# Another order of the calls on five engines, in a kernel of attention and experts on one core of Trainium2

## The reference

```python
xn = layernorm(x)
# attention: 32 query heads, 8 key/value heads, head size 128
q, k, v = heads(xn @ Wq.T), heads(xn @ Wk.T), heads(xn @ Wv.T)
q, k = q * cos + rotate_half(q) * sin, k * cos + rotate_half(k) * sin
attn = softmax(where(causal, q @ k.T / sqrt(128), -inf)) @ v
# experts: 16 of them in 4 groups, the best 2 groups, in them the best 2 experts
s = softmax(xn @ router_w + router_b) + router_bias
gate = scores of the 2 chosen experts, 0 for the others
ffn = sum_e gate_e * ((silu(xn @ w1_e + b1_e) * (xn @ w2_e + b2_e)) @ w3_e + b3_e)
shared = (silu(xn @ sw1 + sb1) * (xn @ sw2 + sb2)) @ sw3 + sb3
out = x + attn @ Wo.T + ffn + shared
```

## Time and profile before

| | |
|---|---|
| median of 3 runs | 904.24 us (903.93 to 904.62) |
| the profiled execution | 904.18 us |
| its span | 902.4 us |
| TensorE busy | 880.4 us, 98% |
| VectorE / POOL / ScalarE busy | 689.3 / 521.7 / 425.6 us |
| chain that ended last, by engine | PE 73%, DVE 9%, issue 5%, DMA 5%, POOL 4% |
| heads, us from the span's start | 74.2, 164.8, 271.2, 377.2, 483.4, 589.6, 695.2, 802.3, end 902.4 |

### The profile page before, as it was taken

How to read it: one execution, slowest core, us unless ns; L and a number is a source line. 1 busy time by engine, 2 the same in 40 slices (tenths; PEclk the granted TensorE clock), 3 DMA queues, 4 the chain that set the end, 5 groups by cost and what they waited for, 6 DMA issues and landing times.

```text
span 902.4 us, 17525 instructions
## 1 busy us (share of the span) xinstructions
PE 880.4 (98%) x5086; PEld 752.5 (83%) x5086; DVE 689.3 (76%) x1615; ACT 425.6 (47%) x1082; POOL 521.7 (58%) x638
## 2 busy tenths in 40 slices
PE   8997999999999999999999999999999999999987
PEld 7786887888888888888888888888888878888766
DVE  5587877777677877778777787778867696787976
ACT  3504544454545544554454455454454554544542
POOL 5915776547554576545754476545756447644564
PEclk9998999999999999999999999999999999999999
DMA  9911122244222532225322343225423153221153
GB/s 332 318 47 47 36 93 94 95 130 140 82 72 76 173 109 85 88 66 178 98 87 79 120 146 102 76 76 152 127 76 87 64 192 99 87 65 48 40 147 106
DMA packets 52161, 97.73 MB, mean 108 GB/s; under 512 B 5920, under 2 KB 17824, under 8 KB 52128
## 3 DMA queue, kind: packets, MB, share of 16 engines
q1 hardware_dynamic: 49568, 88.94, 31.1%
q0 software_dynamic: 2560, 8.39, 2.9%
HBM read 74.76 MB, written 22.54 MB: 108 GB/s over the span
## 4 chain that ended last, share of the span: by engine, by line
PE 73%; DVE 9%; issue 5%; DMA 5%; POOL 4%; ACT 2%; SPq 1%; POOLq 0%; DVEq 0%; ACTq 0%
PE bank L1891 8%; PE bank L1893 8%; PE bank L1892 8%; PE bank L2118 5%; PE bank L2025 5%; PE bank L2122 5%; PE bank L2119 5%; PE bank L2027 5%; PE bank L2026 5%; PE bank L2086 4%; PE bank L2099 3%; PE bank L2102 3%; PE bank L2100 3%; DMA w_raw<-w 2%; POOL prob L586 1%
## 5 line engine op out<-in xcount | busy, mean ns | idle before, releaser
L586 POOL TENSOR_SCALAR prob<-prob,rsum 128x128 f32<-128x128 f32 (+3 forms) x256 | 141.6, 572 | 137.0 <-DVE rsum L1405 136.8
L812 ACT ACTIVATE prob<-bank,nmax 128x128 f32<-128x128 f32 (+3 forms) x256 | 133.6, 528 | 105.8 <-DVE nmax L1399 100.5
L1399 DVE CUSTOM_DVE_ANT_0 bank<-bank,causal 128x128 f32<-128x128 f32 (+3 forms) x256 | 121.0, 507 | 35.3 <-PE bank L1893 26.1
L832 ACT ACTIVATE pT_hi<-bank 128x512 fp32r<-128x512 f32 x160 | 91.6, 596 | 91.6 <-PE bank L2086 76.8
L1427 DVE TENSOR_TENSOR pT_lo<-bank,pT_hi 128x512 fp32r<-128x512 f32 x160 | 105.3, 682 | 26.8 <-ACT pT_hi L832 24.0
L535 POOL TENSOR_TENSOR q_first<-rot 128x128 f32<-128x128 f32 x60 | 28.6, 476 | 138.8 <-DVE rot L1355 138.8
L2025 PE MATMUL bank<-xT_hi,wq_lo 128*128 128x512 f32 x256 | 103.3, 403 | 1.8 <-DVE kT_lo L1390 1.5
L2118 PE MATMUL bank<-wo_lo,oT_hi 128*128 128x512 f32 x256 | 102.8, 402 | 1.7 <-DVE y L1420 1.4
L2027 PE MATMUL bank<-xT_hi,wq_hi 128*128 128x512 f32 x256 | 101.0, 395 | 0.0
L2122 PE MATMUL bank<-wo_hi,oT_lo 128*128 128x512 f32 x256 | 100.9, 394 | 0.0
L2026 PE MATMUL bank<-xT_lo,wq_hi 128*128 128x512 f32 x256 | 100.9, 394 | 0.0
(11 more groups left out here) (219 smaller groups left out, 2341.6 us busy)
## 6 DMA issues: line engine op xcount, KB each, us to landing
w_raw<-w SPq DMA_DIRECT2D x31, 512.0 KB, 4.3
wq_raw<-wq SPq DMA_DIRECT2D x32, 256.0 KB, 2.7
wo_raw<-wo SPq DMA_DIRECT2D x32, 256.0 KB, 3.0
xg<-x_slots SPq DMA_DIRECT2D x31, 256.0 KB, 3.6
w_raw<-w SPq DMA_DIRECT2D x31, 256.0 KB, 2.6
eb<-b SPq DMA_DIRECT2D x31, 256.0 KB, 3.8
y_slots<-eb SPq DMA_DIRECT2D x31, 256.0 KB, 2.4
x_slots<-pairs SPq DMA_DIRECT2D x3, 2048.0 KB, 16.5
```

The costliest lines, as they stand in the source:

```text
L586: last = nc.gpsimd.tensor_scalar(row, row, rsum[:, stat(b, i, h)], 1.0, ALU.mult, ALU.mult)
L812: last = nc.scalar.activation(prob[n % 2][:, h, 0:P * (i + 1)], bank[S_BANKS[use % 2]][:, 256 * k:256 * k + P * (i + 1)], ACT.Exp, bias=nm ...
```

## The change

The same calls stand in another order. In SyncE's and POOL's lists first_head and key_head change (of POOL's last_head the first few calls), in ScalarE's, VectorE's and TensorE's all three lists. No call is added or taken away: key_head has 158 calls on TensorE, 136 on VectorE, 95 on ScalarE, 39 on SyncE and 35 on POOL in both; arguments, buffers and semaphores are the same. The diff, cut to the places that follow:

```diff
@@ POOL, first_head
                         gather(n, 1)
 
             def first_head(g):
-                place_x(g, 0)
                 normalise(g, 0, 0)
                 normalise(g, 0, 1)
                 add_k(g, 1, 0)
                 add_q(g, 1, 0)
                 add_k(g, 1, 1)
+                place_x(g, 0)
+                add_q(g, 1, 1)
                 normalise(g, 0, 2)
-                add_q(g, 1, 1)
+                normalise(g, 0, 3)
...
@@ VectorE, first_head
             def first_head(g):
                 maxima(g, 0, 0, 0)
-                first_places(g, 0)
                 maxima(g, 0, 0, 1)
                 turn_k(g, 1, 0)
+                first_places(g, 0)
                 lo_v(g, 1, 0)
+                maxima(g, 0, 1, 0)
                 inverse_sums(g, 0, 0)
-                maxima(g, 0, 1, 0)
                 maxima(g, 0, 1, 1)
-                lo_wo(g, 0)
+                inverse_sums(g, 0, 1)
                 turn_q1(g, 1, 0)
-                turn_q2(g, 1, 0)
-                inverse_sums(g, 0, 1)
-                lo_wo(g, 1)
-                lo_wo(g, 2)
                 maxima(g, 0, 2, 0)
                 maxima(g, 0, 2, 1)
+                turn_q2(g, 1, 0)
+                maxima(g, 0, 2, 2)
+                maxima(g, 0, 2, 3)
+                lo_wo(g, 0)
                 lo_pT(g, 0, 0, 0)
                 turn_k(g, 1, 1)
+                lo_wo(g, 1)
...
@@ VectorE, key_head
                 lo_pT(g, 0, 1, 1)
-                add_b12(tile_of(g, 1))
-                lo_q(g, 1, 0)
-                maxima(g, 0, 3, 1)
+                lo_xg(tile_of(g, 1))
+                add_out(g - 1, 1, 3)
+                turn_q1(g, 1, 1)
+                turn_q2(g, 1, 1)
                 lo_wo(g, 0)
                 lo_wo(g, 1)
+                add_b12(tile_of(g, 1))
+                maxima(g, 0, 3, 0)
                 expert_product(tile_of(g, 1))
-                turn_q1(g, 1, 1)
-                turn_q2(g, 1, 1)
                 expert_hidden(tile_of(g, 1))
-                add_out(g - 1, 1, 3)
-                maxima(g, 0, 3, 2)
-                lo_kT(g, 1)
-                lo_hT(tile_of(g, 1))
-                lo_q(g, 1, 1)
-                lo_pT(g, 0, 2, 0)
-                maxima(g, 0, 3, 3)
-                add_b3(tile_of(g, 1))
-                lo_oT(g, 0, 1)
                 lo_wo(g, 2)
                 lo_wo(g, 3)
+                lo_hT(tile_of(g, 1))
+                lo_pT(g, 0, 2, 0)
...
@@ VectorE, last_head
-                lo_pT(g, 0, 3, 1)
-                lo_oT(g, 0, 2)
                 maxima(g, 1, 3, 3)
-                add_out(g, 0, 1)
+                combine_two(g, 0)
+                inverse_sums(g, 1, 3)
                 maxima(g, 1, 2, 0)
-                inverse_sums(g, 1, 3)
                 lo_pT(g, 0, 3, 2)
                 maxima(g, 1, 2, 1)
                 lo_pT(g, 0, 3, 3)
-                combine_two(g, 0)
                 maxima(g, 1, 2, 2)
-                maxima(g, 1, 2, 3)
+                add_out(g, 0, 2)
                 lo_oT(g, 0, 3)
                 lo_pT(g, 1, 3, 0)
                 lo_pT(g, 1, 3, 1)
-                add_out(g, 0, 2)
+                maxima(g, 1, 2, 3)
+                combine_two(g, 1)
                 inverse_sums(g, 1, 2)
                 lo_pT(g, 1, 3, 2)
-                combine_two(g, 1)
+                maxima(g, 1, 1, 0)
                 lo_pT(g, 1, 3, 3)
-                lo_pT(g, 1, 2, 0)
-                maxima(g, 1, 1, 0)
                 maxima(g, 1, 1, 1)
                 lo_oT(g, 1, 3)
+                lo_pT(g, 1, 2, 0)
                 lo_pT(g, 1, 2, 1)
+                inverse_sums(g, 1, 1)
                 add_out(g, 0, 3)
-                inverse_sums(g, 1, 1)
                 maxima(g, 1, 0, 0)
+                lo_pT(g, 1, 2, 2)
                 maxima(g, 1, 0, 1)
-                lo_pT(g, 1, 2, 2)
                 combine_two(g, 2)
                 lo_oT(g, 1, 2)
```

More of the change, by code:

```diff
@@ L1661, in key_head @@
                 maxima(g, 0, 2, 2)
+                lo_pT(g, 0, 0, 0)
+                lo_oT(g - 1, 1, 3)
                 maxima(g, 0, 2, 3)
[L1663 to L1668 removed]
+                add_out(g - 1, 1, 2)
+                turn_k(g, 1, 1)
+                lo_q(g, 1, 0)
+                inverse_sums(g, 0, 2)
+                lo_v(g, 1, 1)
@@ new lines, in key_head @@
+                transpose_p(g, 0, 3, 3)
+                project_out(g, 0, 2, 0)
+                project_out(g, 0, 2, 1)
+                project_out(g, 0, 2, 2)
+                scores(g, 1, 1, 0)
+                scores(g, 1, 1, 1)
+                expert_down(tile_of(g, 2))
+                project_out(g, 0, 2, 3)
+                project_q(g + 1, 0, 0, 0)
+                project_q(g + 1, 0, 0, 1)
+                transpose_x(tile_of(g, 3))
+                transpose_p(g, 1, 0, 0)
+                values(g, 0, 3, 2)
```

1143 lines of the change are left out of this document (565 added, 578 removed).

## The result

The changed kernel takes 892.82 us (median of 4 runs, 891.38 to 896.03) where the kernel before, in the same measurement, takes 904.09 (902.66 to 904.62): ratio 0.9883, 95% interval 0.9853 to 0.9912, 11.3 us faster. I had forecast 902.1, with a range from 897.5 to 907.5. The profiled execution has a span of 890.6 us.

What follows compares the result with a forecast made beforehand. TensorE was taken as the bound, busy 880.4 of 902.4 us, leaving at most 22.0 us to reordering. 904.18 + 0.4 (first head) - 0.6 (six passes) - 1.9 (last head) = 902.1 us, range 897.5 to 907.5.

Steps and rivals of the forecast that it cites:

- The first head, +0.4: First head: later lo_v and new waits slightly outweigh taking POOL's scatters off normalise's path; +0.4 us, ends -1.5 and +2.
- The six passes, -0.6: Six middle passes: two waits go, smaller ones come; -0.1 us each, -0.6 in sum.
- the two waits of the middle pass: Middle pass: TensorE's waits for kT_lo (0.40 us) and pT_lo (0.44) go, 0.84 in sum.
- transpose_h(1): Middle pass, tile 1: 5.6 us of matmuls against a VectorE chain of 5.35; 0.3 us taken, 1.1 if one lo_wo is stretched.
- transpose_x(4): Middle pass, tile 4: stands 3.8 us behind what it needs against a chain of 3.65; 0.35 us (0 to 0.7).
- expert_down(0): Middle pass, tile 0: a new lateness of 0.1 us.
- a term that I had put at nothing: Middle pass: merging transpose runs saves nothing, with 13 runs before and after by the orders.
- theory D: Follow-up theory, not in the prediction, on key_head: where TensorE's calls stand (distance) sets the pass, whatever VectorE's operations take.
- rival C: Passes: VectorE falls behind, lo_wo stretched beside POOL's add_q(1,1), from 0.25 us on; 907.2 us, chance 0.25.
- Rival B: Passes: separating VectorE from POOL's subtracts removes every wait, -0.84 us each, idle under 0.2; 897.7 us, chance 0.17.
- The last head, -1.9: Last head: moved combines let inverse_sums(1,1) and normalise come earlier, emptying project_out's 1.36 us wait; -1.9 us.
- Rival D: Whole kernel: nothing gained, the 1.36 us wait moves and passes exchange waits; 904.2 us, chance 0.20.

Runs made afterwards that it cites:

- before_again: The kernel before once more, unchanged: 905.46 us.
- kt_swap: The kernel before with one TensorE swap in key_head, project_q(g,1,2,0) behind expert_down(1): 904.8 us.
- three_more: The changed kernel with three places mended (VectorE's row slots, one project_kv piece, inverse_sums and normalise(1,3) earlier): 887.9 us, ratio 0.9832 to the kernel before.
- pool_hit: The changed kernel with one POOL swap in key_head, lo_w3(1) behind add_q(1,1): 897.24 us.
- key_no_pool: The kernel before with key_head in the new order on four engines, POOL's list kept as before: 942.05 us.
- pool_free: The kernel before with one POOL swap in key_head, lo_w3(2) ahead of split_q(g+1,0): 903.7 us.
- key_only: The kernel before with only key_head in the new order, on all five engines: 898.46 us.

## Why the prediction was wrong

**The first head, +0.4.** Its steps came nearly as written: lo_v ended 0.9 us later, 2.60 us behind turn_k's start where it was 1.69 (at 81.90 in the profile after), the scatters left the path, and one short wait for normalise(0,1) came (0.41, and one of 0.26 in batch 1). Rows of after, to be laid beside the earlier trace rows:

```profile
80.04 0.28 DVE L1319 SCALAR_TENSOR_TENSOR place<-per_expert,bank 128x128 f32<-128x128 f32 x1
...
81.48 0.42 DVE L1383 TENSOR_TENSOR v_lo<-bank,v_hi 128x256 fp32r<-128x256 f32 x1
...
81.95 0.50 PE L2025 MATMUL bank<-xT_hi,wq_lo 128*128 128x512 f32 x1 [1.25 <-DVE v_lo L1383]
...
82.92 1.42 POOL L586 TENSOR_SCALAR prob<-prob,rsum 128x128 f32<-128x128 f32 x4 [7.77 <-DVE rsum L1405]
...
86.95 0.36 PE L2086 MATMUL bank<-ident,prob_t 128*128 128x128 f32 x2 [0.41 <-POOL prob L586]
```

Measured, it is the same as the profile before (90.5 for 90.6 us), and 1.8 less than that order takes on average. What failed is the size of the wait for normalise behind the scatters: I took it from one execution, and that was one of the two in which it was shortest. The granted clock goes with it. From the head's start to the first of these transposes, in the profile before and in before_again:

```profile
74.18:88.01 13.83, 11.47 (x57) 10.20 (x57) 9.41 (x34) 7.71 (x23) 7.45 (x10) 0.75 0.16 66
72.16:86.24 14.08, 10.04 (x57) 8.79 (x57) 10.47 (x36) 7.60 (x23) 7.70 (x10) 0.88 0.16 65
```

Where TensorE ran at 1.2 GHz for 6.8 us of it (before, kt_swap) it came later to the transposes and waited 1.0 us; where it ran so for 3.4 (the six other profiles with the old first head) it waited 2.8 to 3.4 us. Without the wait TensorE would have come 12.1 us behind the head's start in before_again and 13.1 in the profile before: 1.0 of the 1.7 us by which the waits differ.

**The six passes, -0.6.** This is the step that failed. Measured: 106.4 to 105.2, -1.2 a pass, 5.9 us in the five that can be compared, a little over half of the result. It failed in three places. What goes: I counted the two waits of the middle pass, 0.84 us. In the seven profiles of the old key_head the pass also has waits for wo_lo of up to 0.9 us and for kT_lo of up to 0.94 (start to start, above the usual distance), that come and go from pass to pass, and they went too. What comes: I took 0.3 for transpose_h(1), 0.35 for transpose_x(4) and 0.1 for expert_down(0), 0.75 in all. The first two did not come. The third is the one that did, and it costs 0.43 from start to start (lo_hT of tile 0 behind turn_q2(1,0)):

```profile
283.64 0.68 DVE L1355 TENSOR_TENSOR rot<-bank,qs 64x512 f32<-64x512 f32 x1
...
284.36 0.29 DVE L1497 TENSOR_TENSOR hT_lo<-bank,hT_hi 128x128 fp32r<-128x128 f32 x1
...
284.80 0.47 PE L1891 MATMUL bank<-w_hi,hT_lo 128*128 128x512 f32 x1 [0.27 <-DVE hT_lo L1497]
```

The third place is a term that I had put at nothing. I had counted 13 runs of transposes of probabilities before and after; the trace has 13 before (seven of eight, six of four) and 12 after (eight of eight, four of four), and that isn't all. With every wait that the table lists taken out at its length from start to start, a pass of the old order still takes 105.3 to 105.6 us in its seven profiles, one of the new order 104.7, and three_more, whose passes have no such wait, takes 104.8. So 0.5 to 0.9 of the 1.2 us a pass, an estimate, are in no wait of the table. Part of it lies between short matmuls of different kinds: in the profile before transpose_k begins at 361.09, 0.25 us behind the transpose ahead of it, and the second of the scores at 275.58 is 0.18 behind the first, where 0.09 and 0.11 are usual and the middle pass after has nothing longer. This is theory D's side, the places of TensorE's calls; no run takes it apart from the rest.

The two errors on the waits have one root: I had VectorE as stretched after as before. The chain that I reckoned for transpose_h, 5.35 us against 5.6, holds undisturbed; and it was nearly undisturbed.

```profile
299.94 1.56 DVE L1455 TENSOR_TENSOR wo_lo<-wo_raw,wo_hi 128x512 fp32r<-128x512 f32 x2
...
299.99 0.96 POOL L535 TENSOR_TENSOR q_first<-rot 128x128 f32<-128x128 f32 x1 [0.38 <-DVE rot L1355]
...
302.36 0.28 DVE L1480 SCALAR_TENSOR_TENSOR gated<-both_in 128x128 f32<-128x128 f32 x1
...
303.02 0.14 PEld L2167 LDWEIGHTS bank<-ident,h_rows_t 128*128 128x128 f32 x1 [0.17 <-DVE h_rows L1490]
```

This is rival C's place, and it went the other way: VectorE and POOL start at the same signal, VectorE is 0.05 us ahead, and it is POOL's L535 that takes 0.96 us for 0.46; the two lo_wo lose 0.2 us together, under the 0.25 from which C decides. pool_hit shows that C's price was of the right size (1.1 us a pass, once the product is the one that comes second) and its condition not met. Rival B, with 0.17, comes nearest: the stretches beside POOL went from 31.4 to 10.5 us and the waits for pT_lo and kT_lo with them. But its sign, under 0.2 us idle a pass, wasn't met (0.27), and its -0.84 a pass is too small and holds waits alone. How much of the 1.2 us is due to the meetings is not shown: by what is left without the waits they can have about half, key_no_pool mixes two causes, and pool_free shows that a single meeting can be taken away for nothing.

The rule of the Trainium skill that I had set beside row 312.23 ("SBUF — State Buffer", section "Who interferes with whom"), that the engine which comes second is shut out for the whole instruction, is what the 57 stretched operations do. For descriptor writing, which is what a gather does on POOL, the same section infers that it needs another interface than such an operation of VectorE takes; here the gathers took 1.01 us and beside combines 1.21 to 1.63. My reading, that exclusion would cost four whole combines and that the row at 882.77 therefore doesn't agree, was wrong: in the 14 profiles 68 gathers began while such an operation of VectorE ran, and 66 of them ended at its end plus their own shortest 1.01 us, less 0.03 to 0.13. A gather waits for the rest of the one combine that it meets, 0.65 us at 882.77. The other way round there is nothing: of 158 such operations that began beside a scatter or a gather, 150 took less than 0.1 us longer.

**The last head, -1.9.** Measured alone: -2.0, and with the new key head in front of it (198.2 and 199.9 for key_only's 202.0) -3.0 on average. Without the time at 1.2 GHz, by the estimate above, it is -1.0 and -2.1; so that it is in part luck that the measured -2.0 comes so near. The mechanism was right. After, to be laid beside the earlier trace rows:

```profile
858.45 3.12 DVE L1514 SCALAR_TENSOR_TENSOR y<-gath,slot_gate,y 128x512 f32<-128x512 f32 x4
...
868.49 1.84 POOL L586 TENSOR_SCALAR prob<-prob,rsum 128x256 f32<-128x256 f32 x4 [3.72 <-DVE rsum L1405]
...
877.77 0.33 PE L2086 MATMUL bank<-ident,prob_t 128*128 128x128 f32 x2 [1.37 <-POOL prob L586]
...
878.80 0.37 PE L2086 MATMUL bank<-ident,prob_t 128*128 128x128 f32 x2 [0.70 <-POOL prob L586]
```

The combines of 858.45 stand ahead of inverse_sums(1,2) and take 3.12 us for 4.31, normalise(1,1) had waited 3.72 us instead of 7.00 and came 12.3 us earlier in the span (3.7 against the last head's first scores, where I had reckoned 2.2), and project_out waits for no y. Two waits for normalise(1,0) behind the four gathers, 1.37 and 0.70, have come, where the profile before had one of 0.41.

**The prologue.** 2.9 us between the two profiles were chance. The first head begins at 71.0 to 72.2 us in the seven other profiles with the old first head and at 71.0 to 71.3 in the six with the new one, so that a few tenths may be left of it in the medians.

**Rival D** is refuted, and the sign of the forecast was right. The sum as measured: five passes -5.9, all the rest from the first head on -5.1 (293.8 us on average in the two profiles of the changed kernel, 298.9 in the five of the kernel before and its single exchanges), together -11.0 against 11.3. Of the 5.1 some 1.3 are granted clock, 10.2 us at 1.2 GHz for 12.8 on average; whether that follows from the order or is chance isn't settled.

## What to carry to other kernels

Where two engines exclude each other for whole instructions, ask of each operation not how long it takes but who is running when it starts, and compare the sum of what it took with its shortest instance: 31 us of it on VectorE were in sight in the profile before. But don't take the whole gain for it: take the listed waits out of a stage and see whether what is left is the same in both orders. In the old order, with many meetings, three single exchanges moved a wait and brought nothing; in the new one the one wait of the pass that was taken out stayed out. Don't price a wait by one execution: look at how much the same wait differs from pass to pass, and take a second profile if there is one. Before two profiles of a stage are compared, compare the clock that TensorE was granted in it.
